# ScalarE's table set for logarithm and exponential, loaded by name: once at the block's opening and behind each sequence's gating function

## The chip, the cores and the metric

One core of a Trainium2 chip runs the whole program. The metric is the device time of one execution in microseconds; the kernel before was run three times. TensorE (PE) does the matrix products, VectorE (DVE) and GpSimd (POOL) the elementwise work, ScalarE (ACT) the copies with scaling and every function that is read from a table, SyncE (SP) issues transfers.

## The reference, cut to what matters

The model has three stages, and the change touches the last two:

```python
# attention stage: 16 heads of 16, kernel of distances
dist = jnp.maximum(q_norm - 2.0 * qk + jnp.swapaxes(k_norm, -2, -1), 0.0)
scores = jnp.exp(-gamma[None, :, None, None] * SCALE * dist)
...
# window stage: two layers, 8 heads of 64, windows of 128
q = l2norm(q) * qs
k = l2norm(k) * ksc
...
attn = jax.nn.softmax(sim, axis=-1)
...
a, g = jnp.split(h, 2, axis=-1)
h = a * jax.nn.gelu(g, approximate=False)
x = x + h @ w2 + b2
```

The norm of `l2norm` needs one over a square root. The kernel computes it on ScalarE as exp(-0.5 · ln(s)), and one Newton step on VectorE makes it exact enough. So the window stage uses three functions that have tables: logarithm, exponential (also for the softmax) and the gating function gelu.

## The kernel before, in words

First comes the tower phase (a state-space model and a feed-forward net, four layers; gelu on ScalarE at L360). The change leaves it as it is. Behind it one block holds the attention phase and the window phase, joined so that the pipeline of the second fills while the first drains.

The window phase works on 16 pairs of 256 tokens (8 pairs by 2 layers), in software-pipelined "halves": `half(h)` is written once per engine. The half h handles step a of pair h, step b of pair h-1, and so on to step g of pair h-6; `real(x)` is true where a pair has that number. Each engine runs its list in the order in which it is written, and semaphores alone tie the engines together. In half h ScalarE's list holds, in this order: `probabilities` 6 and 7 of pair h-3, squares and copies; `output_hi(2)` of h-3; `probabilities` 0 and 1 of pair h-2; `root(b, 0)`; `probabilities` 2 and 3; six `gelu` of pair h-5; `root(b, 1)`; `output_hi(3)`, `keep_values(b, 0)`, `probabilities` 4 and 5, `spread(a)`, `hidden_hi(f, 0)`, `keep_values(b, 1)`. In some halves a part of a layer's weights is rounded there too: `hi_2(0)` stands ahead of `spread` in half 5, `hi_qkv(2)` behind `keep_values(b, 1)` in half 8.

- `root(n, t)` (L1947, L1949): waits for the sums of squares, takes the logarithm into `w_lg`, then exp(-0.5 x) into `w_y`. VectorE finishes it as `w_rn` (L2167 to L2173).
- `probabilities(k)` (L1963, L1965): two exponentials with a sum along the row. VectorE takes the reciprocal `w_rinv` (L2190), POOL scales by it (L2406, L2407, tile `w_pr`), PE turns the result (L1663, tile `w_ps_p`), and VectorE copies it out (L2196, tile `w_pt`).
- `gelu(f, j)` (L1999) into `w_gate`; VectorE multiplies (L2241), ScalarE rounds (`hidden_hi`, L2006, tile `w_h_hi`), POOL takes the rest (L2411, `w_h_lo`), PE uses both.
- `spread(a)` (L1927, L1928, tile `w_ah`) waits for the turned input and for both value projections of the pair before it (`v_full`); VectorE takes the rest `w_al` (L2134, L2135), and PE projects with both (L1633 to L1635, tile `w_ring`).
- POOL's list has `lo_2` (L2380, L2381) between the first two `hidden_lo` of half 5, and `lo_qkv(2)` (L2390) ahead of a scaling of `w_pr` in half 8.
- The attention phase takes its exponentials in `kernel_exp` (L1060, 128 of them).

```python
def root(n, t):
    act.wait_ge(S["sc_done"], 2 * n + t + 1)
    act.activation(lg[:, t, :, :], sc[:, t, :, :], ACT.Ln).then_inc(S["lg_done"], 1)
    act.wait_ge(S["lg_done"], 2 * n + t + 1)
    act.activation(y0[:, t, :, :], lg[:, t, :, :], ACT.Exp, scale=-0.5).then_inc(S["y0_done"], 1)
```

Of the kernel before, what the change touches and what calls it, by code (L numbers as in the profile page):

```python
# [1388 lines left out]
def window_phase(nc, sems, X, dram, out, raw, qkv, opening, done):  # L1389
# [21 lines left out]
    with ExitStack() as ctx:  # L1411
# [68 lines left out]
        def real(m):  # L1480

            return 0 <= m < M
# [412 lines left out]
        def scalar(act):  # L1895
# [72 lines left out]
            def output_hi(u):  # L1968
                m, c = divmod(u, NU)
                act.wait_ge(S["pv_done"], u + 1)  # L1970
                if c == 0 and m >= 2:
                    act.wait_ge(S["y_full"], m - 1)
                act.activation(ot_hi[:, c, half_of(m)], ps_a[:, 0, 0:STOK], ACT.Copy).then_inc(S["ot_h"], 1)
# [21 lines left out]
            def gelu(f, j, b):  # L1995
                act.wait_ge(S["g_full"], FC // 2 * f + j // 2 + 1)
                if j < DC:
                    act.wait_ge(S["split2"], f + 1)
                act.activation(gate[:, j, :], ring[:, RB[b], j % 2 * STOK:(j % 2 + 1) * STOK], ACT.Gelu,  # L1999
                               bias=b1_all[:, f // NSQ, 1, j:j + 1]).then_inc(S["gelu_done"], 1)  # L2000

            def hidden_hi(f, j):
                act.wait_ge(S["gated"], FC * f + j + 1)
                if FC * f + j >= HS:
                    act.wait_ge(S["h_used"], FC * f + j - HS + 1)
                act.activation(h_hi[:, j % HS, :], gate[:, j, :], ACT.Copy).then_inc(S["h_hi"], 1)  # L2006

            def half(h):
                a, b, c, d, e, f, g = h, h - 1, h - 2, h - 3, h - 4, h - 5, h - 6
                if real(g):  # L2010
                    hidden_hi(g, 1)
                if real(d):
                    output_hi(NU * d + 0)
                if h == 5:
                    hi_1(0, 1)
                if real(b):
                    squares(b, 0, 0, 0)
                if real(g):
                    hidden_hi(g, 2)
                if real(d):  # L2020
                    probabilities(H * d + 6)
                if real(b):
                    squares(b, 0, 1, 1)
                if real(d):
                    probabilities(H * d + 7)
                if real(c):
                    turned(c, 1, 0, 3)
                if real(d):
                    output_hi(NU * d + 1)
                if real(c):  # L2030
                    turned(c, 1, 1, 0)
                if real(b):
                    squares(b, 1, 0, 2)
                if h == 8:
                    hi_qkv(0, "q_full")
                if real(f):
                    norm(f)
                if real(g):
                    hidden_hi(g, 3)
                    hidden_hi(g, 4)  # L2040
                if real(b):
                    turned(b, 0, 0, 0)
                if real(g):
                    hidden_hi(g, 5)
                if h == 13:
                    hi_1(1, 0)
                if real(b):
                    squares(b, 1, 1, 3)
                if h == 8:
                    hi_qkv(1, "k_full")  # L2050
                if real(f):
                    affine(f, 2)
                if h == 5:
                    hi_1(0, 0)
                if h == 11:
                    hi_o(1)
                if real(d):
                    output_hi(NU * d + 2)
                if real(c):
                    probabilities(H * c + 0)  # L2060
                    probabilities(H * c + 1)
                if real(b):
                    root(b, 0)
                if real(c):
                    probabilities(H * c + 2)
                    probabilities(H * c + 3)
                if real(f):
                    gelu(f, 0, 3)
                    gelu(f, 1, 3)
                    gelu(f, 2, 0)  # L2070
                    gelu(f, 3, 0)
                    gelu(f, 4, 2)
                    gelu(f, 5, 2)
                if h == 12:
                    hi_1(1, 1)
                if h == 13:
                    hi_2(1)
                if real(b):
                    root(b, 1)
                if h == 3:  # L2080
                    hi_o(0)
                if real(c):
                    probabilities(H * c + 4)
                if real(d):
                    output_hi(NU * d + 3)
                if real(b):
                    keep_values(b, 0, 3)
                if real(c):
                    probabilities(H * c + 5)
                if h == 5:  # L2090
                    hi_2(0)
                if real(a):
                    spread(a, 0)
                if real(f):
                    hidden_hi(f, 0)
                if real(b):
                    keep_values(b, 1, 2)
                if h == 8:
                    hi_qkv(2, "v_full")
                if real(b):  # L2100
                    turned(b, 0, 1, 1)

            return half, spread

        def vector(dve):

# [408 lines left out]
def program(nc, dram, out, phases=3):  # L2515
# [7 lines left out]
    with ExitStack() as ctx:  # L2523
# [13 lines left out]
        if phases >= 2:  # L2537
            w_sync, w_tensor, w_scalar, w_vector, w_gpsimd = window_phase(nc, sems, X, dram, out, raw, qkv, opening, done)
            with nc.Block() as block:
                M2, M3 = 8, 16  # L2540

                @block.sync
                def _(sp):
                    store = a_sync(sp)
                    prefetch, rest = w_sync(sp)
                    prefetch()
                    for s in range(M2 - 2):
                        store(s)
                    rest()

                @block.tensor
                def _(pe):
                    early_half = a_tensor(pe)
                    half, turn_first = w_tensor(pe)
                    for h in range(M2 + 1):
                        early_half(h)
                    early_half(M2 + 1, turn_first)
                    half(1, lambda: early_half(M2 + 2))
                    for h in range(2, M3 + 6):
                        half(h)  # L2560

                @block.scalar
                def _(act):
                    early_half = a_scalar(act)
                    half, spread = w_scalar(act)
                    for h in range(M2 + 5):
                        early_half(h)
                    early_half(M2 + 5, lambda: spread(0, 0))
                    early_half(M2 + 6)
                    for h in range(1, M3 + 6):  # L2570
                        half(h)

                @block.vector
                def _(dve):
                    early_half = a_vector(dve)
                    half, pads, table, fills, x0_variance, x0_norm, split_in, rotate = w_vector(dve)
                    pads()
                    for h in range(M2 + 4):
                        early_half(h)
                        if h == 2:  # L2580
                            table()
                    x0_variance(0)
                    early_half(M2 + 4, lambda: x0_norm(0))
                    split_in(0, 0)
                    x0_variance(1)
                    rotate(0, 0, 0, 0)
                    early_half(M2 + 5)
                    x0_norm(1)
                    rotate(0, 0, 1, 1)
                    half(1)  # L2590
                    fills()
                    for h in range(2, M3 + 6):
                        half(h)

                @block.gpsimd
                def _(pool):
                    early_half = a_gpsimd(pool)
                    half, masks, x0_root = w_gpsimd(pool)
                    for h in range(M2 + 4):
                        early_half(h)  # L2600
                        if h == 1:
                            masks()
                    early_half(M2 + 4, lambda: x0_root(0))
                    for h in range(M3 + 5):
                        half(h)

            nc.clear_and_free_semaphores(sems)
            nc.all_engine_barrier()
            return
# [27 lines left out]
```

## Time and profile before

| | |
|---|---|
| three runs: median (lowest to highest) | 1358.09 us (1357.83 to 1359.99) |
| the profiled execution: its own time | 1364.02 us |
| its span in the profile | 1362.3 us |
| PE busy | 1244.2 us (91%) |
| VectorE busy | 970.2 us (71%) |
| ScalarE busy | 923.7 us (68%), table loads among it |
| GpSimd busy | 634.2 us (47%) |
| granted PE clock, mean of the span | 0.967 |

The tower fills the first 515 us or so, the attention phase runs to about 700 us, the window phase to the end. The first load for the gating function in the window phase, that of half 5, starts at 829.3 us, and later halves follow 36.6 us apart where nothing holds them up. In the rows below a time in square brackets is how long the engine stood idle ahead of the row, and what released it.

### The profile page before, as it was taken

To read this page: it belongs to the slowest core of one execution; us is meant where nothing else is said; L and a number is where in the kernel's file an instruction comes from. 1 tells how busy PE (TensorE), PEld (TensorE's weight loads), DVE (VectorE), ACT (ScalarE), POOL (GpSimd) and SP (SyncE) were. 2 spreads that over 40 slices of the span, in tenths; PEclk is the share of its full clock that TensorE was granted. 3 is DMA by queue.
4 is the path that set the end of the run, shared out by engine and by line. 5 is a ranking of instruction groups with operands and counts; after the bars stand their busy time and mean duration, and the time that the engine had idled before them with its cause. 6 is when DMAs were issued, how large, how long until landed. Compare 5 with 4: busy or idle time off the path is not lost.

```text
span 1362.3 us, 26380 instructions
## 1 busy us (share of the span) xinstructions
PE 1244.2 (91%) x9057; PEld 1065.0 (78%) x9057; DVE 970.2 (71%) x2602; ACT 923.7 (68%) x2023; POOL 634.2 (47%) x697
## 2 busy tenths in 40 slices
PE   2799999999999993899977888999999999999986
PEld 2699888989988993677755566888788888888876
DVE  5767666666667746898786886778787888877532
ACT  2455765565676642889956778788778788888633
POOL 6523421442343214455334566556556566555523
PEclk9799999999999997999987999999999999999988
DMA  7300010010000004000010002000100000000010
GB/s 170 98 1 14 32 33 1 14 64 1 1 1 1 1 0 115 1 17 14 12 65 1 2 5 87 5 6 5 47 5 6 17 4 13 20 21 21 20 32 16
DMA packets 34881, 33.75 MB, mean 25 GB/s; under 512 B 11340, under 2 KB 31424, under 8 KB 34752
## 3 DMA queue, kind: packets, MB, share of 16 engines
q1 hardware_dynamic: 33856, 29.91, 7.2%
q0 software_dynamic: 768, 2.10, 1.0%
q8 instruction: 79, 1.29, 0.4%
q14 instruction: 50, 0.41, 0.1%
q10 hardware_dynamic: 128, 0.04, 0.0%
HBM read 25.75 MB, written 4.19 MB: 22 GB/s over the span
## 4 chain that ended last, share of the span: by engine, by line
PE 41%; ACT 8%; DVE 4%; POOL 3%; issue 3%; DMA 2%; SPq 1%; ACTq 0%; DVEq 0%; POOLq 0%
PE w_ring L1633 2%; PE w_ring L1635 2%; PE w_ring L1634 2%; PE w_ps_p L1663 2%; PE w_ring L1713 2%; PE a_ps L845 2%; PE w_ring L1714 2%; PE w_ring L1715 2%; PE w_ps_a L1681 2%; PE w_ring L1640 2%; DMA w_xs<-X 2%; PE w_ring L1725 2%; PE w_ps_d L1656 1%; PE w_ps_d L1653 1%; PE w_ring L1726 1%
## 5 line engine op out<-in xcount | busy, mean ns | idle before, releaser
L360 ACT ACTIVATE t_gf<-t_ps_f,t_fb_cur 128x512 f32<-128x512 f32 x128 | 87.9, 687 | 166.0 <-PE t_ps_f L280 164.3
L508 DVE TENSOR_TENSOR t_g_lo<-t_gf,t_g_hi 128x512 fp32r<-128x512 f32 x128 | 94.2, 738 | 81.2 <-ACT t_g_hi L362 80.4
L293 PE MATMUL t_ps_o<-t_w_hi,t_g_hi 128*128 128x256 f32 x512 | 145.9, 285 | 0.9 <-DVE t_g_lo L508 0.9
L295 PE MATMUL t_ps_o<-t_w_hi,t_g_lo 128*128 128x256 f32 x512 | 144.9, 283 | 0.0
L294 PE MATMUL t_ps_o<-t_w_lo,t_g_hi 128*128 128x256 f32 x512 | 144.9, 283 | 0.0
L1713 PE MATMUL w_ring<-w_nh,w_w_hi 128*128 128x256 f32 x384 | 114.5, 298 | 12.8 <-DVE w_gate L2241 6.1
L644 POOL TENSOR_TENSOR t_rs<-t_ve,t_neghalf 128x4 f32<-128x4 f32 x32 | 38.5, 1203 | 181.3 <-DVE t_ve L469 180.0
L2196 DVE COPY w_pt<-w_ps_p 128x384 f32<-128x384 f32 x128 | 70.5, 551 | 60.2 <-PE w_ps_p L1663 59.0
L278 PE MATMUL t_ps_f<-t_nh,t_w_hi 128*128 128x512 f32 x256 | 103.5, 404 | 7.9 <-DVE t_nl L607 3.6
L1714 PE MATMUL w_ring<-w_nh,w_w_lo 128*128 128x256 f32 x384 | 109.2, 284 | 0.0
L1715 PE MATMUL w_ring<-w_nl,w_w_hi 128*128 128x256 f32 x384 | 109.1, 284 | 0.0
L2411 POOL TENSOR_TENSOR w_h_lo<-w_gate,w_h_hi 128x256 fp32r<-128x256 f32 x96 | 69.8, 735 | 80.6 <-ACT w_h_hi L2006 80.2
L2395 POOL TENSOR_TENSOR w_m<-w_m 128x512 f32<-128x512 f32 x64 | 85.4, 1334 | 42.7 <-DVE w_m L2153 42.7
L279 PE MATMUL t_ps_f<-t_nh,t_w_lo 128*128 128x512 f32 x256 | 101.8, 398 | 0.0
L293 PEld LDWEIGHTS t_ps_o<-t_w_hi,t_g_hi 128*128 128x128 f32 x512 | 97.8, 191 | 4.9 <-issue 1.3
L280 PE MATMUL t_ps_f<-t_nl,t_w_hi 128*128 128x512 f32 x256 | 100.8, 394 | 0.0
L294 PEld LDWEIGHTS t_ps_o<-t_w_lo,t_g_hi 128*128 128x128 f32 x512 | 98.0, 191 | 2.6
L295 PEld LDWEIGHTS t_ps_o<-t_w_hi,t_g_lo 128*128 128x128 f32 x512 | 98.0, 191 | 0.0
L1633 PE MATMUL w_ring<-qkv_hi,w_ah 128*128 128x512 f32 x192 | 83.4, 434 | 8.4 <-DVE w_al L2135 5.0
L1713 PEld LDWEIGHTS w_ring<-w_nh,w_w_hi 128*128 128x128 f32 x384 | 74.2, 193 | 14.9 <-DVE w_gate L2241 6.7
L362 ACT ACTIVATE t_g_hi<-t_gf 128x512 fp32r<-128x512 f32 x128 | 80.9, 632 | 4.1
L2406 POOL TENSOR_TENSOR w_pr<-w_pr,w_rinv 128x256 f32<-128x256 f32 x64 | 39.3, 613 | 95.2 <-DVE w_rinv L2190 95.2
(290 smaller groups left out, 4375.4 us busy)
## 6 DMA issues: line engine op xcount, KB each, us to landing
t_raw<-in_L_tok_w SPq DMA_DIRECT2D x8, 1024.0 KB
out<-X SPq DMA_DIRECT2D x14, 256.0 KB, 2.1
raw<-in_L_ffn_wqkv SPq DMA_DIRECT2D x2, 1536.0 KB, 6.8
raw<-in_L_ffn_w SPq DMA_DIRECT2D x4, 682.0 KB, 5.0
w_raw_o<-out SPq DMA_DIRECT2D x8, 256.0 KB, 3.1
w_xs<-X SPq DMA_DIRECT2D x16, 127.0 KB
w_raw<-in_L_ffn_w SPq DMA_DIRECT2D x2, 640.0 KB
t_raw_d<-in_L_tok_D SPq DMA_DIRECT2D x4, 256.0 KB
```

The lines of the kernel that those rows point to most:

```text
L278: pe.matmul(ps_f[:, j % 2, :], w1_hi[:, c, col], nh[1][:, c, :], start=(c == 0), stop=False)
L279: pe.matmul(ps_f[:, j % 2, :], w1_lo[:, c, col], nh[1][:, c, :], start=False, stop=False)
L280: mm = pe.matmul(ps_f[:, j % 2, :], w1_hi[:, c, col], nl[1][:, c, :], start=False, stop=(c == DC - 1))
L293: pe.matmul(out, g_hi[:, j % 4, tok], w2_hi[:, j, :], start=(j == 0 and t % 2 == 0), stop=False, skip_group_check=True)
L294: pe.matmul(out, g_hi[:, j % 4, tok], w2_lo[:, j, :], start=False, stop=False, skip_group_check=True)
L295: mm = pe.matmul(out, g_lo[:, j % 4, tok], w2_hi[:, j, :], start=False, stop=(j == FC - 1 and t % 2 == 1), skip_group_check=True)
L360: act.activation(gf[:, j % 2, :], ps_f[:, j % 2, :], ACT.Gelu, bias=fb_cur[:, j:j + 1]).then_inc(pf_free, 1)
L508: dve.tensor_tensor(g_lo[:, j % 4, :], gf[:, j % 2, :], g_hi[:, j % 4, :].bitcast(F32), ALU.subtract).then_inc(g_split, 1)
L1633: pe.matmul(ring[:, RB[b], :], ah[:, c, tok], qkv_hi[:, c, cols], start=(c == 0), stop=False)
L1713: pe.matmul(dst, w1_hi[:, c, u, cols], nh[:, c, :], start=(j % 2 == 0 and c == 0), stop=False, skip_group_check=True)
L1714: pe.matmul(dst, w1_lo[:, c, u, cols], nh[:, c, :], start=False, stop=False, skip_group_check=True)
L1715: mm = pe.matmul(dst, w1_hi[:, c, u, cols], nl[:, c, :], start=False, stop=(j % 2 == 1 and c == DC - 1), skip_group_check=True)
```

## The change

ScalarE loads the set `natural_log_exp_and_others` by name, once as the first thing of the block, and again right behind the six gating functions of a half, if a root or a probability is still to come in it.

```diff
@@ scalar(act), half(h)
                     gelu(f, 4, 2)
                     gelu(f, 5, 2)
+                    if real(b) or real(c):
+                        act.preload_act_table_set("natural_log_exp_and_others")
...
-            return half, spread
+            def tables():
+
+                act.preload_act_table_set("natural_log_exp_and_others")
+
+            return half, spread, tables
...
                 @block.scalar
                 def _(act):
                     early_half = a_scalar(act)
-                    half, spread = w_scalar(act)
+                    half, spread, tables = w_scalar(act)
+                    tables()
```

Nothing else is edited; every line number behind L2074 grows. On ScalarE, at the block's opening, behind the tower's last rounding of attention weights, the difference between the two orders is:

```order
 L411 ACTIVATE wa_ohi<-raw 128x512
 L59 UNCONDITIONAL_BRANCH
-L2562 UNCONDITIONAL_BRANCH
+L2568 UNCONDITIONAL_BRANCH
+L2107 ACT_TABLE_LOAD
 L1071 ACTIVATE qkv_hi<-raw 128x384 x4
 L1007 ACTIVATE a_nh<-a_ps 128x512
```

The load that stood ahead of the first exponential of the attention phase (L1060) is gone in return.

On ScalarE in half 5, the first with gating functions, the rows from the gating functions to the probabilities behind the second root stood before as

```order
L1999 ACT_TABLE_LOAD
L1999 ACTIVATE w_gate<-w_ring,w_b_all 128x256 x6
L1947 ACT_TABLE_LOAD
L1947 ACTIVATE w_lg<-w_sc 128x16
L1949 ACT_TABLE_LOAD
L1949 ACTIVATE w_y<-w_lg 128x16
L1963 ACTIVATE w_pr,w_rsum<-w_pr,w_mx 128x128
```

and now stand as

```order
L1999 ACT_TABLE_LOAD
L1999 ACTIVATE w_gate<-w_ring,w_b_all 128x256 x6
L2075 ACT_TABLE_LOAD
L1947 ACTIVATE w_lg<-w_sc 128x16
L1949 ACTIVATE w_y<-w_lg 128x16
L1963 ACTIVATE w_pr,w_rsum<-w_pr,w_mx 128x128
```

The load by name takes the place of the logarithm's own, and the exponential's is gone.

On ScalarE, where the first root of that half stands between the probabilities, both loads are gone (the difference, of the half 6 like all later ones):

```order
 L1963 ACTIVATE w_pr,w_rsum<-w_pr,w_mx 128x128
 L1965 ACTIVATE w_pr,w_rsum<-w_pr,w_mx 128x256
-L1947 ACT_TABLE_LOAD
-L1947 ACTIVATE w_lg<-w_sc 128x16
-L1949 ACT_TABLE_LOAD
```

The logarithm follows there at once behind the probabilities. No instruction of another engine moves.

## Rows read from the trace of the kernel before

**Rows 1.** Groups by line, ScalarE: busy us, mean ns, idle before, releaser.
```profile
L1947 ACT ACT_TABLE_LOAD x32 | 41.1, 1283 | 0.6
L1949 ACT ACT_TABLE_LOAD x32 | 41.1, 1283 | 0.6
L1999 ACT ACT_TABLE_LOAD x14 | 18.0, 1283 | 0.2
L1060 ACT ACT_TABLE_LOAD x1 | 1.3, 1283 | 0.0
L1963 ACT ACT_TABLE_LOAD x1 | 1.3, 1283 | 0.0
L1060 ACT ACTIVATE a_e<-a_dist,a_gsc 128x384 f32<-128x384 f32 x128 | 70.1, 622 | 9.9 <-DVE a_dist L1185 8.3 <-PE a_ps L875 0.2
```
**Rows 2.** Stretches: length, busy PE, PEld, DVE, ACT, POOL, PEclk, DMA, GB/s.
```profile
570.00:640.00 70.00, 69.44 (x668) 54.06 (x671) 64.95 (x146) 63.08 (x131) 34.52 (x46) 0.99 0.04 13
780.00:860.00 80.00, 70.15 (x482) 54.34 (x483) 61.80 (x210) 60.89 (x157) 48.96 (x47) 0.96 0.12 40
860.00:940.00 80.00, 80.00 (x621) 68.53 (x621) 63.78 (x195) 65.17 (x170) 48.90 (x49) 1.00 0.02 5
```
**Rows 3.** PE's waits from 740 us on: us in total, times, longest.
```profile
PE w_ps_p L1663 <- DVE w_pt L2196: 8.3, 5, 2.9
PE w_ps_p L1663 <- POOL w_pr L2407: 5.7, 3, 2.6
PE w_ring L1640 <- DVE w_gate L2241: 1.8, 1, 1.8
PE w_ring L1633 <- DVE w_al L2135: 1.5, 3, 0.8
PE w_ring L1713 <- ACT w_v L1934: 0.6, 2, 0.4
```
**Rows 4.** Timeline of ScalarE, first exponential of the attention phase: start, us.
```profile
553.20 1.12 ACT L1060 ACTIVATE a_e<-a_dist,a_gsc 128x384 f32<-128x384 f32 x2 [0.76 <-DVE a_dist L1185]
```
**Rows 5.** Timelines of VectorE and PE in half 3.
```profile
774.75 0.42 DVE L2134 TENSOR_TENSOR w_al<-w_ring,w_ah 128x256 fp32r<-128x256 f32 x1 [0.43 <-ACT w_ah L1928]
...
781.97 0.41 PE L1663 MATMUL w_ps_p<-w_ident,w_pr 128*128 128x128 f32 x2 [2.87 <-DVE w_pt L2196]
```
**Rows 6.** Timelines of VectorE and PE in half 4, and a stretch around its wait.
```profile
800.99 0.18 DVE L2190 RECIPROCAL w_rinv<-w_rsum 128x4 f32<-128x4 f32 x1 [1.45 <-ACT w_pr L1965]
...
801.77 0.41 PE L1663 MATMUL w_ps_p<-w_ident,w_pr 128*128 128x128 f32 x2 [1.25 <-DVE w_pt L2196]
...
800.00:804.00 4.00, 2.75 (x20) 2.07 (x19) 2.40 (x10) 3.94 (x10) 2.01 (x3) 1.00 0.06 17
```
**Rows 7.** Timelines of PE, ScalarE and POOL in half 5, and its half-clock stretch.
```profile
836.25 0.39 PE L1635 MATMUL w_ring<-qkv_hi,w_al 128*128 128x512 f32 x1
...
839.82 0.36 ACT L1927 ACTIVATE w_ah<-w_ring 128x256 fp32r<-128x256 f32 x1
...
840.83 0.73 POOL L2411 TENSOR_TENSOR w_h_lo<-w_gate,w_h_hi 128x256 fp32r<-128x256 f32 x1 [2.76 <-ACT w_h_hi L2006]
...
847.47 0.33 PE L1663 MATMUL w_ps_p<-w_ident,w_pr 128*128 128x128 f32 x1 [2.61 <-POOL w_pr L2407]
...
847.00:852.00 5.00, 4.53 (x20) 2.94 (x21) 2.50 (x6) 0.19 (x1) 3.60 (x4) 0.66 0.70 237
```
**Rows 8.** Timelines of PE and ScalarE in half 8.
```profile
952.03 0.39 PE L1635 MATMUL w_ring<-qkv_hi,w_al 128*128 128x512 f32 x1
...
952.98 0.37 ACT L1927 ACTIVATE w_ah<-w_ring 128x256 fp32r<-128x256 f32 x1
...
960.93 0.33 PE L1663 MATMUL w_ps_p<-w_ident,w_pr 128*128 128x128 f32 x1 [1.85 <-POOL w_pr L2407]
```
**Rows 9.** Timelines of POOL and PE in half 16.
```profile
1252.33 0.73 POOL L2411 TENSOR_TENSOR w_h_lo<-w_gate,w_h_hi 128x256 fp32r<-128x256 f32 x1 [0.44 <-ACT w_h_hi L2006]
...
1254.68 0.44 PE L1663 MATMUL w_ps_p<-w_ident,w_pr 128*128 128x128 f32 x2 [1.27 <-POOL w_pr L2407]
```

## The prediction

> **What bounds the kernel now.** I read the groups by line first, to count loads and price one. Behind the tower ScalarE makes 80 table loads, 1283 ns each: 32 for the logarithm, 32 for the exponential behind it, 14 for the gating function, and one each at L1060 and L1963 [rows 1]. Almost nothing is idle in front of them (0.6 us over 32), so a load costs ScalarE its 1283 ns and little more. Then the stretches. From 860 to 940 us, two whole halves with gating functions, PE is busy 80.00 of 80 us at full clock, ScalarE only 65.17 [rows 2]. There the period of 36.6 us is PE's own, and time given to ScalarE is worth nothing. From 780 to 860 us PE is busy 70.15 of 80 us: there something can be won. Last, the waits, to see who holds PE up behind 740 us: chiefly three lines, transposes of probabilities that wait for VectorE's copy (8.3 us, 5 times) or for POOL's scaling (5.7 us, 3 times), and a projection that waits for `w_al` (1.5 us, 3 times) [rows 3]. ScalarE is named for 0.6 us alone; where it matters, it does so through VectorE and POOL, and I follow each wait back to a place where the engine in between stood idle for ScalarE. That idle time is the cap of what a faster ScalarE gives back.
>
> **What the change removes and adds.** In the changed order there are 28 loads behind the tower: 1 at the opening, 14 for the gating function, 13 behind it by name. So 52 of 80 go, 52 × 1.283 = 66.7 us of ScalarE's time. A half without gating functions loses 4 loads (5.1 us), one with them goes from 5 to 2 (3.8 us). Nothing moves on PE, VectorE, POOL or SP, and no wait or transfer is added.
>
> The ScalarE page that weighs against this is "ScalarE: Activation LUTs", section on table sets, of the Trainium skill: a logarithm followed by an exponential is one load, since one set holds both. By that rule the 32 loads of L1949 would not be there, and the change would be worth 32 loads less. The trace of before differs: both lines have their 32 [rows 1], since the program names no set and each function took one of its own.
>
> *The opening.* One load moves from the first exponential to the start of the block. Where it stood, the exponential behind it still waited 0.76 us for VectorE [rows 4], so it was covered and its going gives 0. Where it stands now, ScalarE waits anyway for the weights of the window phase to arrive; if that cover were gone, it would cost 1.28 us. I take 0.
>
> *Halves 1 and 2.* Eight loads go. PE waits there for VectorE and POOL, which are busy or wait for PE; ScalarE stands in no wait that I found. I take 0.
>
> *Half 3.* VectorE stood idle 0.43 us for `w_ah` [rows 5]. Behind that it has the variance and norm of the next tokens, and then the copy for which PE waits 2.87 us at 781.97. Right ahead of the idle time VectorE had been held by PE, so only 0.43 moves. The bounds are 0 and 2.87; I take 0.4, because VectorE, not ScalarE, is busy for the rest of it.
>
> *Half 4.* VectorE stood idle 1.45 us for probabilities that ScalarE finished late, behind two loads (2.6 us); the copy behind it holds PE up by 1.25 us [rows 6]. That goes whole. Of the three waits for `w_al`, 1.5 us in all with 0.8 as the longest [rows 3], the one of this half (0.43) goes too, since all four loads stand ahead of `spread`. Together 1.7 us; bounds 0.4 and 1.7.
>
> *Half 5.* This is the largest term. `spread` may start when the second value projection is done, whose last matmul starts at 836.25 and ends at 836.64; ScalarE got to it at 839.82, 3.2 us late [rows 7], and three loads less ahead of it (3.8 us) bring it there. POOL's first `w_h_lo` starts 1.0 us behind it, at 840.83, and POOL had stood idle 2.76 us for that, which is less than the 3.2. Behind it on POOL stand the rest of `w2` and the scaling for which PE waits 2.61 us at 847.47. All of that chain is POOL's and moves as one, by 2.8 us; PE's earlier waits for `w_al` (0.8) and for `w_v` lie within this sum, since PE reaches the transpose earlier by them and then waits less. So PE passes the transpose 2.8 us earlier and waits there for 0.8 us instead of 2.61. Second, behind the long wait the clock was at its lower level: the mean of 847 to 852 us is 0.66 [rows 7], which with two levels, 1.2 and 2.4 GHz, is 3.4 us at the lower one, in which 1.7 us of work was done. The wait of 1.25 us in half 4 left the clock at 1.00 [rows 6], and 0.8 us is shorter. I add 1.7. Bounds for the half: 1.0 (only the waits for `w_al` and `w_v`) and 5.3 (these, the whole 2.6 and the clock).
>
> *Half 8.* The second value projection ends at 952.42 and `spread` starts at 952.98 [rows 8]. ScalarE can gain 0.6 us there and not its full 3.8, and the chain behind it, POOL's `lo_qkv(2)` and scaling, gives PE 0.6 of its 1.85 us. Bounds 0 and 1.85.
>
> *Half 12 and half 16.* Of the waits for `w_v` 0.4 is in half 12 [rows 3] and goes. In half 16 POOL stood idle 0.44 us for ScalarE ahead of the scaling that PE waits 1.27 us for [rows 9]; I take 0.4, bounds 0 and 1.3.
>
> *Half 13.* PE's wait of 1.8 us for `w_gate` [rows 3] hangs on a transfer that POOL's additions start, and POOL was let go by PE. I take 0, at most 1.8.
>
> *The other halves and the drain behind 1260 us.* Full PE, or VectorE, POOL and the transfers of `w_xs`: 0. The load behind the gating functions of half 17 stays a load.
>
> The sum: 0.4 + 1.7 + 2.8 + 1.7 + 0.6 + 0.4 + 0.4 = 8.0 us, of 66.7 us removed. It is made against the profiled execution, 1364.0 us, which would become 1356.0; that execution lies 5.9 us above the median of the runs, and I carry the difference over: 1358.1 - 8.0 = **1350.1 us**. The low ends sum to 0 + 0.4 + 1.0 + 0 + 0.4 + 0 = 1.8 us, the high ones to 2.9 + 1.7 + 5.3 + 1.9 + 0.4 + 1.3 + 1.8 = 15.3 us. Not all low ends fall together, so I take 3.3 us as the near edge and 14.0 us as the far one: 1344.1 to 1354.8.
>
> **The rivals.**
> *A, the waits change hands.* Where ScalarE comes earlier, PE and VectorE are the next limit at once: in half 5 PE might wait for a later piece of POOL's chain, and the lower clock might only fall elsewhere. Then the low ends hold: 1.8 us, 1356.3. For it speaks that in every half from 860 to 940 us the same release would change nothing [rows 2]; against it, that VectorE and POOL were idle at the named places, with the chain to PE behind them unbroken.
> *B, the loads do not stay away.* The Trainium skill, "ScalarE activation tables: per-element evaluation and per-set limits", section on table sets in the compiler and the runtime, has the back end place the loads itself, per block. If that step took no notice of the named set, the rows would be those of before and the time 1358.1. The changed order shows 28 loads, which speaks against it.
> *C, slower: the exponential of the named set costs more.* Its place is the attention phase, where 128 exponentials of 622 ns [rows 1] now read another table, and ScalarE is busy 63.08 of 70 us beside a PE with 69.44 [rows 2]. If each took x ns more and all of it fell on the path, that is 0.128 x us; from x = 63 ns (10%) the gain of 8.0 us is eaten, at 20% (124 ns, 15.9 us) the time is 1366. The trace of before shows this function with one table only. The second page named above, in its section on what a function is, says that with the same operands an instruction costs the same whichever table is read. By that rule x is 0 and this rival has no price. No row here shows it.
>
> **How the numbers follow.** Forecast 0.80, A 0.13, B 0.02, C 0.03, other mishaps 0.02. Some 0.2%, 2.7 us, is what a measurement can tell from none. The forecast is faster; A lies within 0.2% at its 1.8 us, but may come out up to 4 us, and I give 0.05 of its 0.13 to faster; B and a small C (0.01) are the same, the rest of C and the mishaps slower. That makes faster 0.85, same 0.11, slower 0.04. The range leaves out most of A, B and C, and the far end beyond 14 us.
>
> **What would show it.** Right: 28 loads behind the tower, and in full halves ScalarE idle for PE in place of the removed loads; the period of full halves still 36.6 us; PE's wait at the transpose of half 5 below 1.2 us and no lower clock behind it; the wait of 1.25 us of half 4 gone; that of half 3 still over 2 us. Wrong: full halves shorter than 36.6 us (ScalarE was on the path after all), exponentials longer than 622 ns in the attention phase (C), or a new wait of PE in half 5 (A).

## The result, and the profile after

| | before | changed |
|---|---|---|
| median of 15 runs each (lowest to highest) | 1359.37 us (1356.03 to 1364.22) | 1355.52 us (1351.63 to 1358.41) |
| ratio of the times, 95% interval | | 0.9967 [0.9954, 0.9979] |
| the profiled execution; its span | 1364.02; 1362.3 us | 1355.29; 1353.6 us |
| ScalarE busy | 923.7 us | 860.4 us |
| PE busy; mean granted clock | 1244.2 us; 0.967 | 1236.8 us; 0.970 |

The change makes the kernel faster, by 0.33% or 4.5 us (2.9 to 6.3). I had said 8.0 us and a time of 1350.1, with 1354.8 as the upper end, so the sign was right and the size was not. Of the 5.4 us between 1350.1 and 1355.5, 1.3 is the base: the median of the three runs that I started from, 1358.1, is that much below the median of 15.

First the loads. These are the groups by line of ScalarE in the changed kernel: busy us, mean ns, idle before.

```profile
L1060 ACT ACTIVATE a_e<-a_dist,a_gsc 128x384 f32<-128x384 f32 x128 | 70.1, 624 | 10.8 <-DVE a_dist L1185 9.2 <-PE a_ps L875 0.2
...
L1999 ACT ACT_TABLE_LOAD x14 | 18.0, 1283 | 0.2
L2075 ACT ACT_TABLE_LOAD x13 | 16.7, 1283 | 0.2
...
L2107 ACT ACT_TABLE_LOAD x1 | 1.3, 1283 | 8.9 <-DVE a_ks L1204 8.9
```

There are 28 behind the tower, as forecast. ScalarE waits 8.95 us ahead of the one at the opening and 4.54 us for a transfer behind it, so it is covered there. An exponential of the attention phase takes 624 ns against 622 before [rows 1]: an exponential read from the named set costs the same within 2 ns. Next, full halves and PE's waits behind 740 us (the length, then busy us of PE, PEld, VectorE, ScalarE, POOL, then PE's granted clock; in the waits us in total, times, longest):

```profile
860.00:940.00 80.00, 80.00 (x619) 68.76 (x618) 62.73 (x201) 59.49 (x171) 47.02 (x48) 1.00 0.02 6
```

```profile
PE w_ps_p L1663 <- DVE w_pt L2202: 7.3, 4, 3.2
...
PE w_ps_p L1663 <- POOL w_pr L2413: 4.5, 4, 2.1
...
PE w_ring L1640 <- DVE w_gate L2247: 1.8, 1, 1.8
...
PE w_ring L1701 <- DVE w_m L2159: 0.7, 1, 0.7
```

PE is still busy 80.00 of 80 us in full halves. The waits for `w_al` and `w_v` [rows 3] are gone, the one for the probabilities of half 4 too, but POOL's scaling still holds PE up for 2.1 us at its longest, where I had 0.8, and there is a new wait of 0.7 us for `w_m`.

**Where the time came from.** Each PE instruction of one trace was paired with the same one of the other, and the difference of the start times taken; where that difference steps, a stretch grew shorter or longer. The steps, in us against the first profile of before, with place names by its times; each kernel was profiled twice:

| stretch of the trace of before | second profile of before | change | change, second profile | forecast |
|---|---|---|---|---|
| half 3, 765 to 782 | 0.01 | -0.33 | -0.23 | -0.4 |
| half 4, 782 to 830 | -1.55 | -1.15 | -1.14 | -1.7 |
| half 5 to its transpose, 830 to 847.5 | 0.01 | -2.12 | -2.12 | -2.8 |
| behind it, 847.5 to 853 (lower clock) | -0.32 | -0.03 | 0.00 | -1.7 |
| half 8, 958 to 965 | 0.01 | -0.44 | -0.47 | -0.6 |
| half 12, 1090 to 1110 | 0.00 | -0.17 | -0.18 | -0.4 |
| half 16, 1250 to 1260 | -0.01 | -0.49 | -0.49 | -0.4 |
| everything else from 765 to 1285 | -0.23 | -0.01 | -0.06 | 0 |
| sum | -2.1 | -4.7 | -4.7 | -8.0 |

The two profiles of the change agree within 0.1 us at each place. Nothing happens between the named halves. Half 4 steps in the second profile of before because of the clock: in the first, and in both of the change, PE is at the lower level from 783.1 to 786.5 us and never idle; in the second of before it is at full clock there, and the stretch lies at 797.9 to 801.3 us instead, just ahead of where PE waits 1.25 us in the first [rows 6] and does not here. Like for like in the clock, the change's step in half 4 is the one against the first profile.

So the sum of 4.7 us is one against the first profile of before; against the second it is 2.6. The 15 runs of each lie between: 3.9 us by the medians, 4.5 by the ratio. That 4.7 comes so near is in part luck. The places and the sizes of the single steps are what the traces show.

The profiled pair differs by 8.7 us, and the other 4 us can't be put down to the change. 1.5 of them had gone by 765 us and 2.5 lie in the drain, whose last 72 us read, in the first and second profile of before and in the change:

```profile
1290.30:1362.30 72.00, 55.07 (x407) 52.28 (x405) 20.16 (x47) 25.70 (x59) 23.09 (x28) 0.89 0.07 23
```

```profile
1284.60:1356.60 72.00, 55.16 (x441) 52.38 (x440) 20.96 (x49) 28.26 (x65) 25.70 (x31) 0.96 0.07 23
```

```profile
1281.60:1353.60 72.00, 55.26 (x428) 52.49 (x426) 20.17 (x47) 26.77 (x61) 25.58 (x31) 0.94 0.08 23
```

The same kernel had a granted clock of 0.89 once and 0.96 the other time, and was 4.0 us shorter the second time. Over many runs the clocks of the two kernels are alike: a mean of 0.969 over the 15 runs of the change, 0.9695 over 29 runs of before that were taken with the first experiments.

**Half 5, where most of the forecast was.** Timelines of the changed kernel, ScalarE, POOL and PE:

```profile
831.43 0.39 PE L1635 MATMUL w_ring<-qkv_hi,w_al 128*128 128x512 f32 x1
831.86 0.60 ACT L1934 ACTIVATE w_v<-w_ring 128x512 f32<-128x512 f32 x1 [1.56 <-PE w_ring L1635]
...
833.54 1.26 ACT L1906 ACTIVATE w_w_hi<-w_raw 128x1280 fp32r<-128x1280 f32 x1
834.70 0.37 ACT L1927 ACTIVATE w_ah<-w_ring 128x256 fp32r<-128x256 f32 x1
...
835.72 0.74 POOL L2417 TENSOR_TENSOR w_h_lo<-w_gate,w_h_hi 128x256 fp32r<-128x256 f32 x1 [0.84 <-ACT w_h_hi L2006]
...
842.37 0.64 PE L1663 MATMUL w_ps_p<-w_ident,w_pr 128*128 128x128 f32 x3 [2.05 <-POOL w_pr L2413]
```

and the 4.5 us behind that transpose, PE's granted clock as the third number from the end:

```profile
842.40:846.90 4.50, 4.50 (x20) 3.02 (x21) 2.50 (x6) 0.20 (x1) 3.11 (x3) 0.62 0.67 229
```

ScalarE now waits 1.56 us for PE's first value projection. From there to `w_ah` it has 2.84 us of its own work, the copy of that projection, two exponentials with their sums and the rounding of w2, so `w_ah` comes no earlier than 834.70, although PE's second projection was done at 833.65. Behind the transpose the clock is 0.62 still.

### The profile page after: what moved, and what is told of

Read it like the earlier page. It is cut to its first block, busy times and chain, and to the rows that moved or that the text cites. A ratio compares the mean times of both kernels' runs of the same rounds, so it can differ in the third digit from the quotient of the medians.

```text
span 1353.6 us, 26327 instructions
## 1 busy us (share of the span) xinstructions
PE 1236.8 (91%) x9057; PEld 1057.9 (78%) x9057; DVE 971.9 (72%) x2602; ACT 860.4 (64%) x1971; POOL 630.2 (47%) x697
## 4 chain that ended last, share of the span: by engine, by line
PE 43%; DVE 6%; POOL 4%; issue 3%; ACT 2%; DMA 2%; SPq 1%; DVEq 0%; ACTq 0%; POOLq 0%
PE w_ps_p L1663 3%; PE w_ring L1713 3%; PE w_ring L1714 3%; PE w_ring L1715 3%; PE w_ring L1633 2%; PE w_ring L1635 2%; PE w_ring L1634 2%; PE w_ps_a L1681 2%; PE a_ps L845 2%; PE w_ps_d L1656 2%; PE w_ps_d L1653 2%; DMA w_xs<-X 2%; PE w_ring L1725 2%; PE w_ring L1640 2%; PE w_ring L1726 1%
## 5 line engine op out<-in xcount | busy, mean ns | idle before, releaser
L644 POOL TENSOR_TENSOR t_rs<-t_ve,t_neghalf 128x4 f32<-128x4 f32 x32 | 35.0, 1094 | 184.3 <-DVE t_ve L469 182.7
```

## The experiments

The theory behind them: the gain lies in halves 4 and 5 and a little in 8, 12 and 16, and full halves are PE's. The numbers e1 to e10 in the headings are those that the expectations use. e1 to e4 share their runs of before (median 1359.38), e5 to e8 others (1361.31), e9 and e10 others again (1360.12); kernels of different groups are compared by their ratios to before, and a trace's steps are again against the first profile of before.

**The opening load alone (e1)**

```diff
-                    if real(b) or real(c):
-                        act.preload_act_table_set("natural_log_exp_and_others")
```

> The named load at the opening stays, the one behind the gating functions is taken out: no loads from the opening to the first gating function, and from there on 14 + 23 + 23 + 1 = 61, as before the change. Theory T (the gain lies where PE waits on a chain of ScalarE, in halves 4 and 5; in half 5 ScalarE then waits for PE's first value projection and takes the rest of the way to `w_ah` from there, so that a load behind the gating functions is covered up to the 1.56 us of that wait): about 3.2 us below before, about 1.2 us above the full change. In the trace: the wait of 1.25 us of half 4 gone; PE's wait at the transpose of half 5 near 2 us, with the lower clock behind it; the waits of halves 8, 12 and 16 as before. Rival R (a gain of each half, from full halves too: what matters is the number of loads): 18 + 1 of the 52 removed loads, so about 1.6 us below before.

1358.62 us, ratio 0.9991 [0.9978, 1.0005]: 1.2 us below before (3.0 at most), which the times can't tell from nothing; it is nearer to rival R's 1.6 than to the theory's 3.2. The trace decides for the theory: -1.21 in half 4, -2.14 in half 5 to the transpose, and 0.03, 0.01 in halves 12 and 16. So 3.3 us are gained there, and the times show a third of it. Half 3's step of -1.65 has a stretch in it that was at the lower clock in before and not here; behind half 5's transpose the clock was at full (-1.55 more), in half 8 at the lower level (+1.57).

**The load behind the gating functions alone (e2)**

```diff
                     half, spread, tables = w_scalar(act)
-                    tables()
```

> The named load behind the gating functions stays, the one at the opening is taken out: halves 1 to 4 have their loads, and half 5 has 4 instead of 5. Theory T: halves 3 and 4 as before; in half 5 ScalarE reaches `w_ah` one load (1.28 us) earlier, and POOL's chain to the transpose with it, so 1.3 us; then the 1.0 us of halves 8, 12 and 16: 2.3 us below before. Rival R (number of loads): 33 of 52, so 2.9 us. The two are too near each other for the times; the trace decides by where the waits of halves 8, 12 and 16 stand: T has them shorter by 0.4, 0.2 and 0.5 us, and nothing between them.

1360.05 us, ratio 1.0009 [0.9994, 1.0023]. Not faster, where the theory had 2.3. In the trace its steps stand again: 0.09 in half 4, -1.28 in half 5 to the transpose (one load's 1.283), then -0.45, -0.20, -0.52 in halves 8, 12 and 16. Behind the transpose of half 5 the clock was at full here too, -1.54. What spoils both times lies elsewhere; the start of the attention phase is one place, below.

**No loads in the window phase (e3)**

```diff
-                act.activation(gate[:, j, :], ..., ACT.Gelu,
+                act.activation(gate[:, j, :], ..., ACT.Identity,
```

(and the load behind it taken out)

> The gating function of the window phase is replaced by an identity with the same bias (the output is another), so that one load at the opening is the only one of the block: 27 loads less than with the change. Theory T: half 5 gains nothing more (ScalarE waits there for PE's value projection, 1.56 us, more than a load), full halves stay at 36.60 us: within 0.5 us of the full change. Rival R (number of loads): 27 more at the same price, 2.4 us below the full change. Rival P (my prediction's size of half 5 was right but for the loads left in it): the transpose of half 5 is reached without the lower clock, 2 to 3 us below the full change.

1355.31 us, ratio 0.9965 [0.9950, 0.9980]: the full change's time within 0.2 us by the medians, with steps that are its own within 0.02 us (from half 5 on -2.13, -0.02, -0.45, -0.20, -0.49). The kernel leaves out the gating function's values, not its time: in L1999 the identity takes 465 ns where the gating function took 480. 27 further loads gave nothing. The rival that counts loads falls, and so does the one that lets the loads left in half 5 explain my miss.

**w2's rest behind the scaling, on top of the change (e4)**

```diff
                 if real(f):
                     hidden_lo(f, 0)
-                if h == 5:
-                    lo_2(0)
                 if real(f):
                     hidden_lo(f, 1)
...
                     scale_p(NU * c + 2)
+                if h == 5:
+                    lo_2(0)
```

> The full change, and in half 5 POOL takes the scaling of the probabilities ahead of the rest of w2 (3.7 us), not behind it. Theory T: the transpose's wait of 2.05 us goes, and with it the stretch at the lower clock behind it, which cost 1.7 us: 3.0 to 3.7 us below the full change. Rival K (the lower clock does not come from that wait, it would fall there anyway): 2.0 us below, granted clock of the 5 us behind the transpose still 0.66. Rival M (the next piece of POOL's list is late in its place, since w2's rest now stands ahead of the third rest of the hidden values and of the rotation): a new wait of PE of 1 to 2 us within the next 10 us, 0 to 1 us below the full change.

1352.03 us, ratio 0.9941 [0.9920, 0.9962], 3.5 us below the full change. The wait is gone and the clock full, in this window behind the transpose:

```profile
840.90:845.40 4.50, 4.50 (x35) 3.65 (x34) 4.46 (x12) 3.05 (x10) 4.50 (x3) 1.00 0.08 10
```

The step of half 5 is -4.33 instead of -2.12, the one behind it -1.60 instead of 0. That the clock stayed up because the wait is gone isn't shown by this: with the single loads it stayed up behind the wait as well.

**Second profiles** of four kernels, to see how each stands in the attention phase's opening.

> The kernel before, unchanged, for a second profile. In the attention phase's opening VectorE scales the rotary tables (L2352) once the small vectors of the window phase have landed; against the block's opening (its memset of `a_neghalf`, L1258) it started after 18.33 us in the profile of before, 17.7 us in those of the full change and its two variants, and 19.7 and 19.8 us in those of the opening load alone and the load behind the gating functions alone. Theory P (the landing belongs to the program, and is the same each time it runs): 18.3 us again, within 0.3. Rival Z (it differs from one execution to the next): anything from 17.7 to 19.9 us.

> The full change, unchanged, for a second profile. Theory P: VectorE scales the rotary tables 17.7 us behind the block's opening again, and PE's wait for `a_xn` behind it stays near 0.7 us. Rival Z: from 17.7 to 19.9 us. For both: the waits of halves 3 to 16 as in the first profile (3.17, none in half 4, 2.05, 1.41, 0.22, 0.79 us) within 0.1 us, since they hang on no transfer; the granted clock of the 5 us behind the wait of half 5 is 0.66 if it follows from the wait, and may be 1.00 if it does not (it was in the run with the opening load alone, behind 2.03 us).

> The opening load alone, unchanged, for a second profile. Theory P: the rotary tables are scaled 19.7 us behind the block's opening again: then 1.5 to 2 us of the window phase's gain are lost in the attention phase's opening, each time. Rival Z: anything from 17.7 to 19.9 us, and the 12 timed runs have the mean of it.

> The load behind the gating functions alone, unchanged, for a second profile. Theory P: 19.8 us again, as with the opening load alone. Rival Z: anything from 17.7 to 19.9 us.

The tables were scaled 18.33 and 18.44 us behind the opening in before, 17.72 and 18.18 in the change, 19.67 and 19.51 with the opening load alone, 19.83 and 19.62 with the other alone. The landing keeps to the program within 0.5 us, not within the 0.3 of theory P: that sets the two late kernels apart, but not before from the change. The late ones come from SyncE's queue, here in before and then in the run with the opening load alone, where an issue of a small vector took 2.23 us:

```profile
530.15 0.89 SPq L1558 DMA_DIRECT2D w_b_all<-in_L_ffn_b  x1
...
533.02 1.27 SPq L1557 DMA_DIRECT2D w_b_all<-in_L_ffn_b  x1
...
536.14 1.71 DVE L2352 TENSOR_TENSOR w_tab<-w_tab,w_raw 128x128 f32<-128x128 f32 x8 [1.98 <-DMA w_b_all<-in_L_ffn_b]
```

```profile
531.89 2.23 SPq L1558 DMA_DIRECT2D w_b_all<-in_L_ffn_b  x1
...
535.13 1.24 SPq L1557 DMA_DIRECT2D w_b_all<-in_L_ffn_b  x1
...
539.21 0.90 DVE L2356 TENSOR_TENSOR w_tab<-w_tab,w_raw 128x128 f32<-128x128 f32 x4 [3.23 <-DMA w_b_all<-in_L_ffn_b]
```

With the load behind the gating functions alone, PE has lost 1.2 and 1.5 us at 600 us since the opening; with the opening load alone 0.3 and 0.0, so the 1.5 to 2 us that were expected to be lost each time were not. For the 2 us that this kernel lacks only a lower mean clock is on record (0.967 over its 12 runs, 0.9695 over the 29 of before; 0.968 with the other load alone). That part stays open.

**Three rests later on POOL, with the change (e5) and without it (e6)**

```diff
-                if h == 3:
-                    lo_o(0)
...
                 if h == 3:
                     x0_root(3)
+                    lo_o(0)
...
-                if h == 8:
-                    lo_qkv(2)
                 if real(c):
                     scale_p(NU * c + 2)
+                if h == 8:
+                    lo_qkv(2)
```

(and `lo_2(0)` as above)

> The full change, and on POOL three pieces of weight rounding behind the step that PE or VectorE waits for: in half 3 wo's rest (2.4 us) behind the root of the next tokens' variance, in half 5 w2's rest behind the scaling (as in e4), in half 8 a third of wqkv's rest (2.4 us) behind the scaling. Theory T: beside the 3.5 us of e4, PE's wait of 1.41 us in half 8 goes, and VectorE's idle time of 1.13 us for the root in half 3, so that PE waits there 2.0 us and not 3.17: 1348 to 1350 us, 9.5 to 11 us below before. Rival M (the moved rests are late where they are used, or the next wait takes the place): within 1 us of e4, 1351 to 1353.

e5: 1354.14 us, ratio 0.9949 [0.9932, 0.9967], 6.9 us below before where 9.5 to 11 were expected, and 1.1 us above e4 by the ratios. Half 8 came as expected (step -2.06, its wait gone), half 3 did not. In that half POOL, VectorE and PE read

```profile
775.89 1.02 POOL L2378 TENSOR_TENSOR w_x_rs<-w_x_ve,w_neghalf 128x4 f32<-128x4 f32 x1 [2.15 <-DVE w_x_ve L2125]
776.88 2.35 POOL L2382 TENSOR_TENSOR w_wo_lo<-w_raw_o,w_wo_hi 128x1024 fp32r<-128x1024 f32 x1
776.94 3.41 DVE L2135 TENSOR_SCALAR X<-X,w_x_mv,w_x_rs 128x256 f32<-128x256 f32 x4 [1.13 <-POOL w_x_rs L2378]
780.51 0.61 POOL L2412 TENSOR_TENSOR w_pr<-w_pr,w_rinv 128x256 f32<-128x256 f32 x1 [1.28 <-DVE w_rinv L2196]
...
782.38 0.88 PE L1663 MATMUL w_ps_p<-w_ident,w_pr 128*128 128x128 f32 x3 [4.89 <-DVE w_pt L2202]
```

The wait is 4.89 us instead of 3.17. The root did not come earlier: VectorE waits 1.13 us for it as before, since it starts when VectorE's own variance is there. Nor is POOL late for the scaling, it stands idle 1.28 us for VectorE ahead of it. It is VectorE that is late. In the change its four steps with the root read

```profile
776.73 1.38 DVE L2135 TENSOR_SCALAR X<-X,w_x_mv,w_x_rs 128x256 f32<-128x256 f32 x4 [1.13 <-POOL w_x_rs L2378]
```

and here they take 3.41 us. The first of the four takes 2.44 us (it takes 0.41 to 0.42 in every kernel in which the rest stands elsewhere); it starts 0.06 us behind POOL's rest of 2.35 us and ends 0.15 us behind it. In e6 and e7, with the same order on POOL, it takes 2.44 us again. So here one instruction of VectorE lasted as long as the one of POOL beside it. What couples the two no run here tests.

> The kernel before, all its table loads in place, with the same three moves on POOL. Theory T (loads and POOL's rests stand in the same chain in half 5, and the wait of 2.61 us there goes by either; only what PE waits for `w_al`, `w_v` and the probabilities of half 4 needs the loads gone): 2.6 us and the lower clock's 1.5 in half 5, 1.9 in half 8, 0.8 to 1.1 in half 3: 6 to 7 us below before, 3 to 4 us above e5. Rival S (the chains do not overlap; what the loads give comes on top in full): 4.5 us above e5.

e6: 1356.75 us, ratio 0.9972 [0.9958, 0.9987], 3.8 us below before where 6 to 7 were expected, and 2.6 us above e5, 3.1 by the ratios. What is missing against before is in half 3, which is 2.0 us longer by the same stretched step of VectorE, and behind it in half 4, 1.2 us, where the stretch at the lower clock is longer (6.8 us for 3.4). In the trace half 5 steps by -2.77 and -1.60 without the change, by -4.37 and -1.60 with it. The waits before the transpose need ScalarE's loads gone, the transpose's own goes by either.

**ScalarE's rounding of w2 earlier, on top of the run with three rests (e7)**

```diff
+                if h == 5:
+                    hi_2(0)
                 if real(b):
                     keep_values(b, 0, 3)
...
-                if h == 5:
-                    hi_2(0)
                 if real(a):
                     spread(a, 0)
```

> As e5, and in half 5 ScalarE's own rounding of w2 (1.56 us) stands ahead of `keep_values(b, 0)`, where it waits 1.56 us for PE, not between it and `spread`. Theory T (in half 5 what was left of ScalarE's lateness at `w_ah` was its own work behind the value projection, 2.84 us of it): `w_ah` comes up to 1.5 us earlier, bounded by the second value projection; PE's wait of about 0.7 us for `w_al` there goes, 0.3 to 1.0 us below e5. Rival N (PE was not held there any more): within 0.2 us of e5; the trace decides, the times can't.

1352.34 us, ratio 0.9939 [0.9921, 0.9956], 1.4 us below e5 by the ratios, within the noise of six runs each. Half 5 steps by -4.33, against -4.37 without it: the rival was right, PE was not held there any more.

**Six more loads in full halves (e8)**

```diff
+                        if h >= 6:
+                            for _ in range(3):
+                                act.preload_act_table_set("gelu_and_others")
+                                act.preload_act_table_set("natural_log_exp_and_others")
```

> The full change with six more loads (7.7 us) behind the named one in each half with gating functions from half 6 on, 2.6 times what the change took out of one. Theory T (full halves are PE's, ScalarE is idle for some 10 of 36.6 us): the loads stand ahead of `root(b, 1)` and of the probabilities that POOL and PE wait for, and ScalarE was idle only 2 to 3 us between them and `spread`; so the period grows, but by less than the 7.7 us: 2 to 5 us a half over 10 to 12 halves, 20 to 60 us slower than the full change. Rival F (the slack of the whole half counts, wherever the loads stand): no change, within 2 us.

1417.81 us, some 62 above the full change (61 by the ratios), just over the theory's 60. The added loads (36 on each of two lines), and PE, which now waits for the value copy in these halves (its waits from 880 to 1300 us, one of them in the timeline, and the stretch itself, whose clock is the third number from the end):

```profile
L2078 ACT ACT_TABLE_LOAD x36 | 46.2, 1283 | 0.2
```

```profile
PE w_ring L1713 <- ACT w_v L1934: 35.9, 11, 4.6
```

```profile
922.03 0.38 PE L1713 MATMUL w_ring<-w_nh,w_w_hi 128*128 128x256 f32 x1 [2.87 <-ACT w_v L1934]
```

```profile
880.00:1300.00 420.00, 384.75 (x2800) 325.23 (x2800) 289.65 (x911) 339.99 (x811) 226.92 (x232) 0.95 0.04 13
```

62 over 12 halves is 5.2 us each for 7.7 us of loads, but not all of it is ScalarE's lateness. The 11 waits are 3.3 us each, and the rest goes with the clock, 0.95 in this stretch where the full halves of the change have 1.00. So the place behind the gating functions has between 2.5 and 4.4 us to give (7.7 less 5.2 or 3.3), two or three loads, and not the 9 us for which ScalarE is idle in a half (59.49 of 80 us busy, above): what counts is where a load stands.

**The rounding of w2 earlier, alone on top of the change (e10)** (the edit on `hi_2(0)` above, POOL's list as in the change)

> The full change, POOL's list as it is, and ScalarE's rounding of w2 (1.56 us) of half 5 ahead of `keep_values(b, 0)`. Theory T (the chain of half 5 starts at `w_ah`, which waited for 2.84 us of ScalarE's own work behind the value projection, 1.5 us of it this rounding): POOL's first `w_h_lo` comes 1.1 to 1.5 us earlier against PE's value projection, PE's wait at the transpose is 0.5 to 1.0 us instead of 2.05, the clock of the 5 us behind it 1.00: 2.5 to 3.2 us below the full change. Rival V (another work is next in the chain at once, VectorE's or PE's): the wait stays over 1.7 us, within 0.5 us of the full change. Rival C (the wait falls, the lower clock stays or comes elsewhere): 1.0 to 1.5 us below.

1354.89 us, ratio 0.9945 [0.9925, 0.9964]: 3.0 us below the full change by the ratios, but the two medians, 1354.89 and 1355.52, are 0.6 apart and the nine runs spread over 9 us. The trace carries this one. It is the missing piece of half 5:

```profile
832.22 1.26 ACT L1906 ACTIVATE w_w_hi<-w_raw 128x1280 fp32r<-128x1280 f32 x1
...
835.59 0.39 ACT L1927 ACTIVATE w_ah<-w_ring 128x256 fp32r<-128x256 f32 x1 [0.42 <-PE w_ring L1635]
...
843.38 0.55 PE L1663 MATMUL w_ps_p<-w_ident,w_pr 128*128 128x128 f32 x3 [1.21 <-POOL w_pr L2413]
```

```profile
843.40:847.90 4.50, 4.50 (x34) 3.64 (x35) 3.69 (x10) 2.25 (x7) 3.16 (x3) 1.00 0.67 228
```

Now `w_ah` waits for PE's second projection, which is the bound that I had taken. The steps are -3.00 to the transpose and -1.57 behind it. The wait at the transpose is 1.21 us, above the 0.5 to 1.0 that were expected: POOL is no longer idle ahead of its first `w_h_lo`, so what is left of the chain is POOL's own work.

**The three rests on POOL, wo's behind the scaling too (e9)**: the change, `lo_2(0)`, `lo_qkv(2)` as above, and `lo_o(0)` of half 3 behind `scale_p(NU * c + 2)`.

> As e5, but in half 3 wo's rest (2.4 us) stands behind the scaling of the probabilities, where POOL waits 2.4 us for VectorE, not between the root and that scaling (there it took PE's wait from 3.17 to 4.89 us). Theory T: half 3's wait at the transpose falls to 2.0 us or by at least the 1.13 us that VectorE waited for the root, half 5's and half 8's waits are gone as in e4 and e5: 5.0 to 6.0 us below the full change, 9.5 to 10.5 below before. Rival M (PE waits in half 3 for VectorE's own work, 3.1 us of it between the cleared root and the copy): half 3 gives nothing, 4.5 to 5.0 us below the full change.

1349.64 us, ratio 0.9925 [0.9903, 0.9947], the fastest of all: 10 us below before, 5.7 below the change by the ratios. That is the theory's range, but in half 3 the rival holds: the wait fell to 2.87 us only, not to 2.0. Against the change half 5 gives 3.8 us (1.6 of it the clock), half 8 gives 1.6. Half 4 has a wait of 1.52 us instead of 0.95. It isn't the price of the moved rest: the second profile of before, with nothing moved, has 1.59 there, and in both PE was at full clock some 13 us ahead of that wait, where before and the change were at the lower one, and so it came there earlier.

```profile
795.75 0.52 PE L1663 MATMUL w_ps_p<-w_ident,w_pr 128*128 128x128 f32 x3 [1.59 <-DVE w_pt L2196]
```

## Why the prediction was right in sign and too large

*Loads, prices, full halves.* 28 loads, 1283 ns, exponentials at their old price, a period that stayed PE's: as predicted, and seen at both ends by taking 27 more loads away (0.2 us) and adding 72 (62 us, clock included). On rival C the Trainium skill, "ScalarE activation tables: per-element evaluation and per-set limits", section on what a function is, says that an instruction costs the same whichever table is read; 624 against 622 ns agrees. The Trainium skill, "ScalarE: Activation LUTs", section on what a load costs, adds a drain of some 1380 ns to each switch of set. The trace has none, ahead of the load or behind it; in half 5 of the change ScalarE reads

```profile
825.08 2.30 ACT L1999 ACTIVATE w_gate<-w_ring,w_b_all 128x256 f32<-128x256 f32 x6
827.40 1.28 ACT L2075 ACT_TABLE_LOAD   x1
828.69 0.21 ACT L1947 ACTIVATE w_lg<-w_sc 128x16 f32<-128x16 f32 x1
```

*Half 5, the chain: 2.8 forecast, 2.1 measured.* This is the first failed step: "`spread` may start when the second value projection is done", and "three loads less bring it there". On ScalarE's queue `keep_values(b, 0)`, probability 5 and `hi_2(0)` stand between a wait for the first projection and `spread`, 2.84 us of work; I took the last condition of `spread` for its ready time and passed over a wait further up its own queue. With `hi_2(0)` out of the way (e10) the chain moves 3.0 us, where I had 2.8.

*Half 5, the clock: 1.7 forecast, 0 measured.* This is the second failed step: that 0.8 us is shorter than the 1.25 us of half 4, which left the clock at 1.00, and so the clock would stay up. With a wait of 2.05 instead of 2.61 the clock was 0.62 again, in both profiles and in the run without loads. The size of the term was right (1.54 to 1.60 wherever the lower clock was absent). Its condition, a wait of 0.8 us, was not met, and the clock is no matter of this wait's length alone: see below. What decides it stays open.

*Half 4: 1.7 forecast, 1.15 measured.* The wait of 1.25 went whole and the 0.43 for `w_al` too. Then PE waits 0.70 us for `w_m`, where VectorE is behind with its own work, not idle. I had not asked what is late next there; rival A's mechanism, in one half.

*Halves 3, 8, 12, 16:* 0.3, 0.45, 0.2, 0.5 for 0.4, 0.6, 0.4, 0.4. Half 3's wait became 3.17, not below 2.87, as predicted for a wait that VectorE's work sets. Half 8's fell by 0.44 for the 0.6 of idle time that I had read.

The two half-5 terms (2.4 us) and half 4 (0.55) are nearly all of the 3.3 us between the sum and the 4.7 measured. As a gain, 4.5 us lies within the 3.3 to 14.0 that the range was made of; as a time, 1355.5 lies 0.7 us above its end, because the base of three runs was 1.3 us low and I had given it no width. A better base would have put the time inside the range with both steps of half 5 still wrong.

## What to carry over

Idle time of the engine behind a late one caps what can be won, but the ready time of a step is that of the slowest thing ahead of it on its own queue, waits included: go up the queue until the first instruction that will itself wait for somebody once the load is gone, and add the work between. A removed cost pays where it stands: 33 of the 52 loads lay in halves 6 to 16 and gave 1.1 us together, while two pieces of POOL's work, each moved behind the scaling that PE waits for, gave 3.8 (1.6 of it the clock) and 1.6 us on top. Before work is moved to where its engine is idle, see what the other engines do beside it: wo's rest, moved beside VectorE's steps in half 3, made PE's wait there 1.7 us longer. Book a clock term only as a second case with a chance of its own, and check a base of three runs against the scatter (here 8 us over 15).

## What the runs showed that I had not expected

The granted clock does not follow from the wait ahead of it. Behind the transpose of half 5 it was 0.62 after a wait of 2.61 in before and 1.00 after one of 2.61 with the load behind the gating functions alone (both times); 0.62 after 2.05 in the change, 1.00 after 2.03 with the opening load alone, both times each. The rows of the last two (the second profile of the change, and the first of the other):

```profile
843.90:848.40 4.50, 4.50 (x20) 2.92 (x21) 2.49 (x6) 0.17 (x1) 3.12 (x3) 0.62 0.68 232
```

```profile
844.10:848.60 4.50, 4.46 (x33) 3.61 (x34) 3.62 (x10) 1.47 (x3) 3.21 (x3) 1.00 0.73 248
```

At this place the clock came out the same in both profiles of each of four kernels. At others it did not: half 8's clock fell in one profile of the opening load alone and stayed up in the other, and half 4 and the drain of before differ between its two. Whether the pattern belongs to the program, two profiles each can't tell. That makes 1.5 us steps which no engine's list explains, and differences of a few us between kernels can be this and nothing else. Why it falls where it does, I can't say from these traces.

The second is SyncE's queue: small transfers of L1557 and L1558 that mostly take 0.38 to 0.50 us to issue take 1.1 to 2.4 us at one or two places of the row, although SyncE's own list is the same in all kernels. An issue of 2.0 to 2.4 us stands in both profiles of each of the two kernels with a single load, and in no other profile. The shorter ones are less steady: the last but one of these eight issues takes 0.38 us in the first profile of the change and 1.27 in the second. What holds the queue there was not tried.
